# A two-layer decoder on one core: the order in which each engine takes the two lanes' pieces

## Chip, cores and metric

One core of a Trainium2 chip runs the whole program in one launch. Time is device microseconds of that core. The kernel before took 1565.3 us (median of 3 runs, 1559.88 to 1567.16).

## What is computed

Four sequences (batch 4, 512 tokens, width 128, float32) go through six sub-layers, each followed by a residual and a layer norm:

```python
x = _layernorm(x + mamba(x, ...))             # 256 channels, 16 states, scan over 512 tokens
x = _layernorm(x + cross_attention(x, ctx))   # 16 heads, 32 context tokens
x = _layernorm(x + experts(x, ...))           # shared + top 2 of 8 experts, hidden width 512
x = _layernorm(x + window_attention(x, ...))  # 16 heads of 8, band of 128, rotary
x = _layernorm(x + cross_attention2(x, ctx))
x = _layernorm(x + local_layers(x, ...))      # two layers: windows of 64, 8 heads of 64, gated GELU feed-forward of width 341
```

## The kernel before

The four sequences are handled by two *lanes* of code, lane 0 and lane 1. Each has its own scratch, its own four of the eight PSUM banks and its own semaphores. Each lane does two sequences one after the other, called row 0 and row 1 of the lane. So at any time two sequences are under way, and the engines work for both.

For each engine there is one generator per stage and lane: `mamba_*`, `cross_*`, `experts_*`, `window_*`, `cross_*` again and `local_*` twice (l = 0 and 1), with `_tensor` (TensorE, "pe"), `_scalar` (ScalarE, "act"), `_vector` (VectorE, "dve") and `_pool` (GpSimd). `row_sync` issues the loads and stores of a lane from the sync queue ("sp"). Each `yield` ends a *piece*: mostly one operation with the waits ahead of it, sometimes a handful. Over the whole program the two lanes have 806 and 840 pieces on TensorE, 665 and 666 on ScalarE, 836 and 869 on VectorE, 91 and 90 on GpSimd, 43 and 33 on the sync queue.

An engine executes its instructions in the order in which they are written. `interleave` writes that order: it reads `TURNS[engine]`, takes so many pieces of lane 0, then so many of lane 1, and so on:

```python
lanes, done = (first, second), object()
last = [next(lanes[k % 2], done) for k, n in enumerate(turns) for _ in range(n)]
```

Inside a lane the order of the pieces is fixed. Between the lanes it is only `TURNS`. The waits (`wait_ge`) stand inside the pieces, so the data is right under any order that doesn't lock up, but an engine whose next instruction waits does nothing for the other lane either.

Places that the sections below name by line:

- Lane 1 begins with the set-up: `setup_tensor` (L545, L549, and L557, L566, L574, L579 for the folded products of the cross attentions), `setup_vector` (L499, L506, L518, L520 copy the results out, L526 to L535 make constants and tables).
- `mamba_tensor`: projections L684, L688, L694, L701, L708, then for each of 16 states L720 (spread B and C) and L731 (sum). `mamba_vector`: L826 (scale by the root), L837 and L839 (convolution), L847 to L855 (split of B and C in three parts), L859 to L864 (step sizes), then for each state L875 (product) and twice L883 (scan). `mamba_scalar`: L784 (Exp), L787 (Ln), L804 (Exp of each state), L811.
- `local_tensor`: projections L1541, transposes L1430, scores L1582 and L1584, L1597 (transposed weights), L1614 and L1616 (heads), L1549 and L1558 (out). Then the feed-forward: L645 (transposes, in a helper that every stage uses), L1627 (mean), L1630 (mean of squares), L1637 and L1640 (gate and value, three pairs), L1644 and L1652 (down). `local_scalar`: L1522 and L1523 (hT), L1725 (Square), L1727 (Ln), L1730 (Exp), L1736 (Gelu). `local_vector`: L1830 and L1831 scale the normed rows.

Of the kernel before, what the change touches and what calls it, by code (L numbers as in the profile page):

```python
# [103 lines left out]
        5, 21, 4, 3, 1, 10, 2, 5, 4, 4, 2, 1, 6, 2, 3, 3, 3, 3, 3, 3, 5, 3, 3, 3, 3, 3, 3, 3, 3, 5, 3, 3, 3, 3,  # L104
        2, 4, 1, 2, 1, 6, 4, 2, 3, 1, 4, 1, 6, 1, 1, 3, 2, 11, 1, 2, 1, 1, 2, 2, 4, 1, 4, 11, 15, 1, 1, 2, 2, 2,
        3, 5, 6, 6, 6, 1, 1, 17, 17, 1, 3, 1, 1, 9, 3, 6, 2, 3, 3, 1, 11, 5, 1, 2, 3, 1, 2, 5, 6, 6, 6, 6, 6, 6,
        6, 6, 1, 6, 3, 6, 3, 1, 5, 3, 6, 3, 1, 5, 5, 6, 6, 4, 5, 2, 2, 6, 2, 7, 1, 2, 5, 4, 4, 2, 4, 4, 3, 4, 1,
        1, 2, 5, 6, 1, 2, 7, 6, 1, 2, 3, 6, 2, 1, 2, 4, 5, 2, 2, 1, 4, 7, 3, 2, 2, 1, 4, 2, 2, 2, 4, 6, 2, 2, 1,
        2, 5, 2, 4, 3, 3, 1, 2, 1, 1, 1, 1, 1, 2, 1, 1, 5, 2, 2, 3, 3, 2, 1, 3, 5, 1, 2, 7, 6, 2, 2, 2, 5, 2, 2,
        2, 4, 5, 2, 2, 1, 4, 7, 3, 5, 7, 3, 5, 5, 2, 4, 6, 2, 4, 3, 3, 1, 2, 1, 1, 1, 1, 1, 2, 1, 1, 5, 3, 2, 2,  # L110
        3, 5, 4, 1, 1, 4, 4, 4, 1, 1, 5, 2, 3, 3, 3, 3, 3, 3, 3, 3, 3, 3, 3, 3, 5, 3, 3, 4, 3, 1, 1, 2, 2, 1, 3,
        3, 3, 3, 4, 3, 1, 1, 1, 2, 1, 5, 4, 1, 2, 1, 8, 1, 1, 5, 3, 3, 2, 8, 1, 1, 2, 2, 5, 1, 4, 11, 14, 1, 2,
        2, 2, 4, 3, 2, 6, 7, 6, 2, 1, 16, 17, 1, 3, 1, 1, 9, 3, 6, 2, 3, 3, 1, 11, 5, 1, 2, 3, 1, 2, 5, 1, 6, 3,
        6, 3, 1, 2, 5, 4, 1, 3, 3, 2, 2, 1, 1, 3, 3, 2, 2, 1, 1, 3, 3, 2, 2, 1, 1, 5, 3, 1, 3, 3, 3, 2, 2, 1, 1,
        3, 3, 2, 2, 1, 1, 5, 5, 5, 1, 2, 5, 2, 7, 1, 2, 5, 4, 4, 2, 4, 4, 3, 4, 1, 1, 2, 5, 8, 6, 2, 2, 4, 2, 2,
        2, 5, 2, 2, 2, 4, 5, 2, 2, 1, 4, 7, 3, 5, 7, 3, 5, 5, 2, 4, 6, 2, 4, 3, 3, 1, 1, 1, 1, 1, 1, 1, 2, 1, 2,
        3, 3, 2, 2, 1, 2, 1, 3, 3, 1, 1, 3, 1, 4, 6, 6, 2, 2, 2, 5, 2, 2, 2, 4, 5, 2, 2, 1, 4, 7, 3, 5, 7, 3, 5,
        5, 2, 4, 6, 2, 4, 3, 2, 1, 1, 1, 2, 1, 1, 1, 2, 1, 2, 3, 3, 2, 2, 2, 2, 3, 3],
    "act": [
        3, 1, 3, 1, 9, 1, 2, 1, 1, 3, 2, 2, 2, 1, 2, 5, 5, 1, 1, 1, 3, 1, 1, 2, 1, 1, 2, 2, 1, 1, 2, 2, 1, 1, 2,  # L120
        1, 1, 3, 2, 3, 1, 1, 2, 2, 1, 1, 2, 2, 1, 1, 1, 2, 1, 1, 2, 1, 1, 2, 2, 1, 1, 2, 2, 1, 1, 12, 3, 2, 9,
        1, 2, 11, 1, 2, 6, 7, 11, 3, 1, 1, 2, 3, 4, 4, 4, 1, 1, 11, 7, 1, 5, 6, 5, 2, 5, 3, 7, 5, 4, 5, 5, 7, 5,
        4, 7, 5, 4, 12, 5, 4, 5, 5, 7, 5, 4, 7, 5, 2, 3, 2, 6, 14, 3, 1, 3, 2, 3, 3, 3, 3, 2, 5, 4, 1, 5, 3, 3,
        6, 5, 5, 4, 2, 8, 4, 1, 8, 4, 1, 6, 3, 2, 4, 1, 5, 3, 1, 5, 3, 1, 6, 1, 1, 1, 1, 1, 1, 1, 1, 1, 1, 4, 4,
        4, 1, 5, 3, 3, 6, 5, 5, 4, 2, 8, 4, 1, 8, 4, 1, 8, 4, 1, 8, 3, 1, 5, 3, 1, 6, 1, 1, 1, 1, 1, 1, 1, 1, 1,
        1, 4, 4, 2, 1, 3, 1, 2, 3, 1, 2, 3, 1, 1, 3, 1, 2, 5, 1, 1, 1, 2, 1, 1, 2, 1, 1, 2, 2, 1, 1, 3, 2, 1, 1,
# [31 lines left out]
        1, 1, 1, 1, 1, 1, 1, 1, 1, 1, 1, 1, 1, 1, 1, 1, 2, 1, 1, 1, 1, 1, 2, 3, 2, 1, 2, 2, 2, 3, 1, 2, 2, 2, 3,  # L158
        3, 1, 1, 2, 1, 1, 1, 1, 2, 1, 1, 2, 2, 1, 1, 1, 2, 1, 1, 1, 1, 1, 1, 1, 1, 1],
    "sp": [  # L160
        11, 1, 2, 1, 3, 1, 4, 1, 1, 2, 4, 9, 1, 1, 1, 1, 2, 1, 3, 1, 4, 2, 1, 1, 4, 11, 2],
}


# [1968 lines left out]
```

## Time and profile before

| | us |
|---|---|
| median of 3 runs (lowest, highest) | 1565.3 (1559.88, 1567.16) |
| span of the profiled execution, first to last instruction | 1544.1 |
| TensorE busy | 1269.2 (82%) |
| VectorE busy | 1046.3 (68%) |
| ScalarE busy | 808.2 (52%) |
| GpSimd busy | 395.7 (26%) |

For the profiled execution the profile gives the span alone; what a run has around it (start and end of the program) isn't in it. The median is 21.2 us longer than that span. The stages of lane 0 in row 0 begin, by TensorE's first instruction of each, near 13 (Mamba), 203 (cross attention), 248 (experts), 351 (window attention), 494 (second cross attention), 527 and 661 us (local layers); row 1 begins near 800 us. Lane 1 enters Mamba at 68 us and the same later stages 5 to 26 us after lane 0, in the last layer of row 1 1 us before it. A busy TensorE isn't one at full speed: the clock granted to it is given beside it as a share of 2.4 GHz, and 0.5 is its lower level.

### The profile page before, as it was taken

To read this page: it belongs to the slowest core of one execution; us is meant where nothing else is said; L and a number is where in the kernel's file an instruction comes from. 1 tells how busy PE (TensorE), PEld (TensorE's weight loads), DVE (VectorE), ACT (ScalarE), POOL (GpSimd) and SP (SyncE) were. 2 spreads that over 40 slices of the span, in tenths; PEclk is the share of its full clock that TensorE was granted. 3 is DMA by queue.
4 is the path that set the end of the run, shared out by engine and by line. 5 is a ranking of instruction groups with operands and counts; after the bars stand their busy time and mean duration, and the time that the engine had idled before them with its cause. 6 is when DMAs were issued, how large, how long until landed. Compare 5 with 4: busy or idle time off the path is not lost. (4 is left out here: it accounts for less than half of the span.)

```text
span 1544.1 us, 23279 instructions
## 1 busy us (share of the span) xinstructions
PE 1269.2 (82%) x8400; PEld 815.4 (53%) x8400; DVE 1046.3 (68%) x2162; ACT 808.2 (52%) x2180; POOL 395.7 (26%) x248
## 2 busy tenths in 40 slices
PE   5767878887998888789775888889689988988986
PEld 4412335884665556456531233579456654655663
DVE  4789976226887787378449998741378879746853
ACT  2466423453764556466627553336276636665663
POOL 0036633412000332032011665360400023202300
PEclk9789978997999989999987888989799999999997
DMA  8300001780000100001010000068400000000000
GB/s 298 123 0 1 0 1 54 254 268 19 2 1 1 35 21 15 1 15 28 2 28 0 1 0 1 1 201 263 130 1 2 1 1 22 22 1 14 22 8 14
DMA packets 42179, 72.21 MB, mean 47 GB/s; under 512 B 3793, under 2 KB 27473, under 8 KB 41810
## 3 DMA queue, kind: packets, MB, share of 16 engines
q1 hardware_dynamic: 28242, 56.30, 10.8%
q10 hardware_dynamic: 11776, 10.23, 2.6%
q0 software_dynamic: 2048, 4.20, 0.9%
q8 instruction: 68, 1.11, 0.3%
q14 instruction: 45, 0.37, 0.1%
HBM read 51.19 MB, written 13.24 MB: 42 GB/s over the span
## 5 line engine op out<-in xcount | busy, mean ns | idle before, releaser
L912 POOL TENSOR_TENSOR scratch<-scratch 128x1024 f32<-128x1024 f32 x64 | 149.7, 2353 | 140.4 <-DVE scratch L883 119.9
L634 POOL TENSOR_TENSOR small<-small,w_const 128x16 f32<-128x16 f32 x32 | 101.1, 3163 | 298.2 <-DVE small L1753 298.2
L731 PE MATMUL psum<-scratch,w_const 128*128 128x512 f32 x256 | 148.8, 713 | 18.5 <-POOL scratch L912 18.4
L883 DVE TENSOR_TENSOR_SCAN scratch<-psum,scratch 128x512 f32<-128x512 f32 x128 | 150.1, 1206 | 9.5 <-ACT psum L804 8.9
L634 POOL TENSOR_TENSOR rstd<-rstd,w_const 128x4 f32<-128x4 f32 x32 | 32.8, 1029 | 432.9 <-DVE rstd L596 430.3
L1706 ACT ACTIVATE scratch<-psum,mx 128x128 f32<-128x128 f32 x256 | 90.0, 376 | 72.7 <-DVE mx L1794 71.5
L804 ACT ACTIVATE psum<-scratch,a_neg 128x512 f32<-128x512 f32 x128 | 87.8, 690 | 61.2 <-DVE scratch L883 52.1
L1374 ACT ACTIVATE scratch<-psum,mx 128x256 f32<-128x256 f32 (+1 forms) x256 | 111.2, 465 | 10.0 <-DVE mx L1410 8.4
L720 PE MATMUL psum<-scratch,cb 96*128 96x512 bf16 x128 | 49.7, 428 | 60.6 <-DVE scratch L875 51.3
L1160 ACT ACTIVATE scratch<-psum,scratch 128x128 f32<-128x128 f32 x240 | 68.3, 368 | 54.7 <-PE psum L1101 54.6
L1541 PE MATMUL psum<-w_local,hT 128*128 128x512 f32 x192 | 91.2, 615 | 6.3 <-ACT hT L1523 5.1
L731 PEld LDWEIGHTS psum<-scratch,w_const 128*128 128x128 f32 x256 | 53.5, 221 | 79.7 <-issue 45.2
L1243 DVE COPY scratch<-psum 128x128 f32<-128x128 f32 x60 | 17.4, 291 | 109.1 <-PE psum L1115 109.1
L875 DVE TENSOR_TENSOR scratch<-scratch,psum 128x1024 f32<-128x1024 f32 x64 | 76.4, 1198 | 4.0 <-PE psum L720 3.7
L1794 DVE TENSOR_REDUCE mx<-psum 128x4 f32<-128x512 f32 x64 | 44.0, 689 | 51.2 <-PE psum L1584 51.1
L1101 PE MATMUL psum<-scratch,expert_weights 128*128 128x128 f32 x480 | 65.5, 280 | 15.3 <-DMA expert_weights<-in_expert_weights 10.8
L1410 DVE TENSOR_REDUCE mx<-psum 128x4 f32<-128x1024 f32 (+1 forms) x56 | 67.9, 1216 | 9.1 <-PE psum L1321 9.1
L720 PEld LDWEIGHTS psum<-scratch,cb 96*128 96x128 bf16 x128 | 13.4, 105 | 114.0 <-DVE scratch L875 75.4
L1584 PE MATMUL psum<-scratch 64*64 64x128 f32 x512 | 71.7, 281 | 0.0
L1582 PE MATMUL psum<-scratch 64*64 64x128 f32 x512 | 71.7, 281 | 0.0
L1303 PE MATMUL psum<-w_const,scratch 128*128 128x128 f32 x448 | 69.4, 284 | 0.9 <-DVE scratch L1400 0.9
L1101 PEld LDWEIGHTS psum<-scratch,expert_weights 128*128 128x128 f32 x480 | 58.2, 192 | 20.1 <-DMA expert_weights<-in_expert_weights 14.1
(266 smaller groups left out, 3199.6 us busy)
## 6 DMA issues: line engine op xcount, KB each, us to landing
expert_weights<-in_expert_weights SPq DMA_DIRECT2D x61, 512.0 KB, 5.1
scratch<-scratch ACTq DMA_DIRECT2D x48, 128.0 KB, 2.3
folded_products<-expert_weights SPq DMA_DIRECT2D x8, 512.0 KB, 3.1
folded<-folded_products SPq DMA_DIRECT2D x8, 512.0 KB, 4.7
w_local<-in_local SPq DMA_DIRECT2D x1, 3122.0 KB
sorted_y<-scratch ACTq DMA_DIRECT2D x12, 256.0 KB, 5.6
scratch<-sorted_x SPq DMA_DIRECT2D x4, 704.0 KB, 6.7
scratch<-in_cross SPq DMA_DIRECT2D x1, 2624.5 KB, 12.9
```

Source lines behind the costliest of these rows:

```text
L634: t.eng.tensor_tensor(v, v, W("const", "neg_half").to_broadcast([P, v.shape[1]]), ALU.pow).then_inc(t.s[done], 1)
L731: ins = pe.matmul(sum_banks[c], ident, t.m.hC[:, 2 * ((n - 1) % 2) + c, :], start=(n == 1), stop=(n == NS))
L804: act.activation(t.ps["dA"], t.m.delta[:, c, :], ACT.Exp, scale=a_neg[:, c, n:n + 1])\
L875: dve.tensor_tensor(t.m.dBu[n % 2], t.m.du[:, :, :], bank, ALU.mult).then_inc(t.s["v_freed"], 1)
L883: dve.tensor_tensor_scan(t.m.hs[:, n % 2, c, :], t.ps["dA"], t.m.dBu[n % 2][:, c, :], 0.0, ALU.mult, ALU.add)\
L912: t.eng.tensor_tensor(t.m.hC[:, 2 * (n % 2):2 * (n % 2) + 2, :], t.m.hs[:, n % 2], C, ALU.mult)\
L1101: ins = pe.matmul(tok(bank, f), t.m.weights[b % BUFS][:, f * P:(f + 1) * P], tok(t.m.xsT, b), start=(f == 0), stop=(f == NF - 1), skip_gro ...
L1374: ins = act.activation(t.m.wide_pr[:, n % 2, u, z], bank[:, z], ACT.Exp, bias=t.m.mx2[:, c:c + 1], accum_out=t.m.sums2[:, c:c + 1])
L1541: pe.matmul(ring.open(), tok(t.m.hT, i), w_qkv[:, c * 512:(c + 1) * 512], start=True, stop=True).then_inc(t.s[sig], 1)
L1582: pe.matmul(own[0:64, :], qs[:, 0:64], ks[:, q - before:q - before + P], start=False, stop=False, skip_group_check=True)
L1584: ins = pe.matmul(own[64:P, :], qs[:, 64:P], ks[:, q:q + P], start=False, stop=(g == 3), skip_group_check=True)
L1706: ins = act.activation(tok(t.m.pr[:, u, :], a), tok(bank, a), ACT.Exp, bias=t.m.mx2[:, c:c + 1], accum_out=t.m.sums2[:, c:c + 1])
```

## The change

All five lists of `TURNS` are replaced. The new ones were made by a procedure that goes through time and lets each engine take, of the pieces that are ready, the one with the longest chain of work behind it, with a preference between the lanes that depends on the stage. The kernel holds only its result. The pieces, their instructions, waits, buffers and banks are as before. The lists add up to the same number of pieces for each lane. The number of runs (entries) goes from 511 to 738 for "pe", 435 to 604 for "act", 714 to 894 for "dve", 131 to 132 for "pool" and 27 to 36 for "sp". The first entries of each list, before and after:

```diff
--- before.py
+++ after.py
 TURNS = {
     "pe": [
-        5, 21, 4, 3, 1, 10, 2, 5, 4, 4, 2, 1, 6, 2, 3, 3, 3, 3, 3, 3, 5, 3, 3, 3, 3, 3, 3, 3, 3, 5, 3, 3, 3, 3,
-        2, 4, 1, 2, 1, 6, 4, 2, 3, 1, 4, 1, 6, 1, 1, 3, 2, 11, 1, 2, 1, 1, 2, 2, 4, 1, 4, 11, 15, 1, 1, 2, 2, 2,
-        3, 5, 6, 6, 6, 1, 1, 17, 17, 1, 3, 1, 1, 9, 3, 6, 2, 3, 3, 1, 11, 5, 1, 2, 3, 1, 2, 5, 6, 6, 6, 6, 6, 6,
...
+        5, 34, 4, 1, 1, 4, 2, 3, 1, 1, 3, 1, 5, 2, 3, 3, 3, 3, 3, 3, 2, 1, 1, 2, 5, 3, 3, 3, 2, 1, 1, 2, 2, 2,
+        1, 3, 3, 2, 1, 1, 2, 3, 3, 3, 2, 3, 1, 3, 1, 5, 1, 1, 4, 1, 5, 1, 1, 3, 1, 1, 1, 1, 4, 3, 2, 1, 1, 7, 1,
+        2, 1, 1, 6, 1, 1, 3, 1, 3, 2, 5, 9, 2, 1, 1, 2, 1, 2, 1, 2, 3, 2, 1, 1, 1, 1, 3, 2, 1, 1, 1, 3, 1, 1, 4,
...
     "act": [
-        3, 1, 3, 1, 9, 1, 2, 1, 1, 3, 2, 2, 2, 1, 2, 5, 5, 1, 1, 1, 3, 1, 1, 2, 1, 1, 2, 2, 1, 1, 2, 2, 1, 1, 2,
-        1, 1, 3, 2, 3, 1, 1, 2, 2, 1, 1, 2, 2, 1, 1, 1, 2, 1, 1, 2, 1, 1, 2, 2, 1, 1, 2, 2, 1, 1, 12, 3, 2, 9,
...
+        4, 2, 5, 1, 4, 2, 1, 2, 2, 1, 1, 1, 1, 3, 2, 2, 1, 1, 4, 1, 1, 2, 3, 2, 1, 1, 3, 1, 2, 2, 2, 1, 1, 2, 2,
+        2, 1, 2, 1, 1, 1, 2, 1, 1, 2, 3, 1, 1, 2, 2, 1, 1, 3, 3, 2, 1, 1, 2, 2, 1, 1, 1, 1, 1, 1, 1, 1, 1, 1, 1,
...
     "dve": [
-        6, 12, 1, 1, 1, 8, 4, 1, 1, 1, 1, 1, 1, 1, 1, 4, 1, 3, 1, 3, 2, 1, 3, 5, 4, 5, 1, 1, 1, 3, 2, 1, 1, 1,
-        2, 1, 1, 2, 2, 1, 1, 2, 2, 1, 1, 2, 2, 1, 1, 1, 1, 1, 1, 1, 1, 2, 2, 1, 1, 2, 2, 1, 1, 2, 1, 1, 1, 2, 1,
-        1, 2, 2, 1, 1, 2, 2, 1, 1, 2, 2, 1, 1, 1, 4, 1, 2, 2, 2, 1, 1, 1, 1, 2, 1, 1, 1, 2, 1, 4, 1, 3, 1, 2, 1,
...
+        7, 20, 1, 15, 3, 2, 6, 1, 1, 1, 1, 1, 1, 1, 3, 5, 2, 1, 1, 3, 2, 1, 1, 1, 1, 1, 1, 2, 1, 1, 2, 1, 1, 1,
+        1, 1, 2, 2, 1, 1, 1, 1, 1, 1, 1, 1, 1, 1, 1, 1, 1, 1, 2, 2, 1, 1, 1, 1, 1, 2, 2, 1, 1, 1, 1, 1, 1, 1, 1,
+        1, 1, 1, 1, 1, 1, 1, 1, 1, 1, 1, 1, 1, 1, 1, 1, 1, 1, 1, 1, 4, 1, 3, 2, 1, 1, 1, 1, 2, 2, 1, 2, 1, 1, 1,
...
     "pool": [
-        3, 2, 5, 1, 1, 1, 1, 1, 1, 1, 1, 1, 1, 1, 1, 1, 1, 1, 1, 1, 1, 1, 1, 1, 1, 3, 2, 1, 1, 1, 2, 2, 1, 1, 1,
...
+        3, 2, 4, 1, 1, 1, 1, 1, 1, 1, 1, 1, 1, 1, 1, 1, 1, 1, 1, 1, 1, 1, 1, 1, 1, 1, 1, 3, 1, 1, 2, 2, 2, 1, 1,
...
     "sp": [
-        11, 1, 2, 1, 3, 1, 4, 1, 1, 2, 4, 9, 1, 1, 1, 1, 2, 1, 3, 1, 4, 2, 1, 1, 4, 11, 2],
+        10, 1, 2, 1, 1, 1, 5, 2, 2, 1, 1, 2, 3, 5, 1, 2, 2, 2, 1, 1, 1, 1, 5, 1, 2, 1, 1, 2, 1, 1, 2, 1, 1, 6,
+        2, 2],
 }
```

## Rows read from the trace of the kernel before

**Rows 1.** The page: busy us of each engine; TensorE's busy tenths and clock in slices

```profile
PE 1269.2 (82%) x8400; PEld 815.4 (53%) x8400; DVE 1046.3 (68%) x2162; ACT 808.2 (52%) x2180; POOL 395.7 (26%) x248
...
PE   5767878887998888789775888889689988988986
...
PEclk9789978997999989999987888989799999999997
```

**Rows 2.** Busy time by stage: stretch, its length, then the engines, clock, DMA share, GB/s

```profile
64.00:192.00 128.00, 94.12 (x219) 35.07 (x220) 118.52 (x116) 74.42 (x117) 69.06 (x31) 0.89 0.02 9
...
192.00:260.00 68.00, 52.33 (x201) 30.22 (x200) 47.42 (x136) 21.00 (x34) 21.39 (x17) 0.80 0.00 1
...
351.00:371.00 20.00, 14.61 (x44) 8.56 (x44) 10.77 (x59) 4.07 (x7) 8.22 (x9) 0.57 0.10 27
...
371.00:496.00 125.00, 117.95 (x1066) 80.14 (x1067) 98.51 (x269) 81.82 (x305) 1.01 (x1) 1.00 0.01 2
...
496.00:532.00 36.00, 29.00 (x134) 17.43 (x133) 26.26 (x75) 12.68 (x22) 11.40 (x11) 0.91 0.05 15
...
787.00:806.00 19.00, 9.84 (x38) 5.61 (x37) 10.10 (x40) 4.39 (x18) 4.55 (x6) 0.73 0.20 55
...
806.00:950.00 144.00, 109.30 (x243) 41.27 (x242) 134.49 (x132) 81.63 (x123) 70.20 (x30) 0.81 0.00 0
...
1102.00:1121.00 19.00, 13.39 (x40) 8.04 (x41) 10.31 (x56) 2.99 (x5) 8.34 (x9) 0.55 0.11 28
...
1121.00:1247.00 126.00, 119.33 (x1076) 80.61 (x1073) 97.96 (x272) 80.81 (x307) 1.01 (x1) 1.00 0.01 1
```

**Rows 3.** The same view in steps of 10 us, local layers of row 0

```profile
630.00:640.00 10.00, 5.86 (x21) 2.74 (x20) 1.66 (x3) 6.84 (x11) 0.00 (x0) 1.00 0.01 2
...
640.00:650.00 10.00, 6.78 (x10) 2.85 (x11) 3.29 (x6) 4.54 (x6) 0.00 (x0) 0.66 0.00 0
...
760.00:770.00 10.00, 3.90 (x11) 1.33 (x9) 2.15 (x4) 7.69 (x11) 0.00 (x0) 0.91 0.00 0
```

**Rows 4.** Timeline of TensorE, row 0's first local layer: start us, us, what

```profile
629.40 0.66 PE L645 MATMUL psum<-w_const,x 128*128 128x128 f32 x4
...
643.22 2.07 PE L1637 MATMUL psum<-scratch,w_local 128*128 128x512 f32 x2 [5.18 <-DVE scratch L1831]
...
655.01 1.02 PE L1640 MATMUL psum<-scratch,w_local 128*128 128x512 f32 x2
```

**Rows 5.** Chain of waits in the last local layer: start us, us, what

```profile
1497.49 0.60 PE psum L645 x4
...
1503.22 0.59 ACT hT L1523
...
1503.83 1.28 ACT L1727
...
1509.68 2.08 PE psum L1637 x2
```

**Rows 6.** Groups of ScalarE by form: line, operation, count, busy us, mean ns

```profile
L1727 ACT ACT_TABLE_LOAD x6 | 7.7, 1283 | 0.1
...
L771 ACT ACT_TABLE_LOAD x1 | 1.3, 1283 | 0.0
```

**Rows 7.** Timeline of TensorE at the start

```profile
37.80 3.53 PE L694 MATMUL psum<-scratch,w_mamba 128*8 128x512 f32 x4
...
43.14 1.98 PE L708 MATMUL psum<-scratch,w_mamba 8*128 8x512 f32 x4
...
58.33 1.05 PE L579 MATMUL psum<-scratch,expert_weights 128*128 128x128 f32 x8
```

**Rows 8.** Timeline of VectorE at the start

```profile
43.25 0.69 DVE L847 CAST scratch<-psum 96x512 bf16<-96x512 f32 x1 [4.66 <-PE psum L701]
...
63.94 0.27 DVE L535 TENSOR_SCALAR w_rows<-w_rows,gate 1x128 f32<-1x128 f32 x1
```

**Rows 9.** Timeline of all engines between row 0 and row 1

```profile
800.05 1.08 PE L645 MATMUL psum<-w_const,y 128*128 128x128 f32 x4 [8.22 <-DVE y L826]
```

105 rows, old and new, of the table TURNS are left out of this document.

## The prediction

> **What bounds the kernel now.** I read the page first [rows 1]: TensorE is busy for 1269.2 of 1544.1 us and VectorE for 1046.3. No engine is full over the whole span, so the question is where TensorE's missing 274.9 us lie. The digits show them in the first eighth, just past the middle, and in notches between stages. The windows cut by stage say why [rows 2]. In the first Mamba stretch VectorE works 118.5 of 128 us and in the second 134.5 of 144: VectorE is the bound there, and no order of turns wins more than its idle 9.5 us in each. In row 0's window attention TensorE works 118.0 of 125 us at full clock: 7 us to win. The idle sits in the seams: 15.7 of 68 us around the first cross attention, 5.4 of 20 and 5.6 of 19 us where lane 0 has begun the window attention and lane 1 has not (there the granted clock is 0.57 and 0.55, close to the lower level of 1.2 GHz, because TensorE has one lane's chain alone), 7 of 36 us around the second cross attention, and 9.2 of 19 us between row 0 and row 1.
>
> Finer windows [rows 3] show the same in the gated feed-forward at the end of each local layer: 5.9 of 10 us busy, then 6.8 at a clock of 0.66; in the second layer 3.9 of 10. The timeline of TensorE [rows 4] shows both lanes there at once: lane 0's transposes (L645) start at 629.40, but its first matmul of the feed-forward (L1637) only at 643.22, and takes 2.07 us a pair where a later pair of that width takes 1.02. The chain of waits in the last layer [rows 5] gives such a chain almost undisturbed: 1497.49 to 1509.68, 12.2 us of short steps with two table loads in it. All this is latency of two lanes standing in the same narrow place together.
>
> **What the change does to the order.** No instruction is altered, so I merged the two lanes' pieces by both tables and named each piece by its line. The number of runs goes from 511 to 738 on TensorE, 714 to 894 on VectorE, 435 to 604 on ScalarE, 131 to 132 on GpSimd and 27 to 36 on the sync queue. A turn costs no instruction. What counts is how far the lanes are shifted. Summing the traced busy time of lane 1's pieces that stand ahead of each lane 0 piece, the two orders differ by at most 8 us on TensorE outside the last layer and by 12 to 16 us within it. It is the same plan with small shifts, so I expect tens of microseconds at the very most.
>
> **Start.** Before, TensorE does 21 set-up pieces, then lane 0's projections L694 to L708, then the rest. After, all 34 set-up pieces come first. On VectorE 14 of the 35 set-up pieces used to be mingled with lane 0's L847 to L864; now all come ahead of them. TensorE's set-up ends at 58.33 + 1.05 = 59.4 [rows 7]; lane 0's projections (37.80 to 43.14 + 1.98 = 45.12, 7.3 us) leave it, so it ends near 52, and L694 slips from 37.80 to 52: 14 us later. VectorE's set-up ended at 63.94 + 0.27 = 64.2 [rows 8] with about 9 us of lane 0's work inside; now near 57. Lane 0's L847 slips from 43.25 to 57, its first scan from 65 to about 72, and lane 1 starts 7 us sooner. From 57 on VectorE has 118.5 + 9 = 127.5 us to do plus some 6 us of idle while both chains start (before, it idled 9.5): 57 + 127.5 + 6 = 190.5 against 192. I take -1 us; bounds -7 (no idle) and +14 (the slip of L694 isn't made good).
>
> **First cross attention and experts.** After, lane 1 is 4 to 8 us of work further on when lane 0 enters, so the two chains run beside each other rather than one after the other. The idle is 15.7 us in row 0 [rows 2]; I take a quarter of it, -4, and -1 for row 1, where the lanes were closer already. Bounds: 0 and -16. The lone-lane stretch before lane 1's window attention follows from lane 1's lag: it enters the experts about 4 us sooner, worth its idle share and the slow clock, -3 in row 0 and -1 in row 1. Bounds: +5 and -11 (both idles).
>
> **Window and second cross attention.** Here 1.7 to 6.4 us less of lane 1's work stands ahead of lane 0's pieces, so its latency-bound cross attention lies beside lane 1's last window units. Idle is 7 us around it [rows 2]: -2 in each row, bounds 0 and -7. Where TensorE was already full, finer turns give nothing.
>
> **Feed-forward of the local layers.** This is the largest shift. In row 0's first layer seven of lane 1's attention pieces (5.4 us on TensorE) that stood ahead of lane 0's L645 now stand behind it, inside lane 0's 12.2 us chain; then lane 0's 10.4 us of L1637 to L1652 stand inside lane 1's chain. Worked from the start of L645: it moves from 629.4 to 624. Chain 12.2, lane 0's matmuls with lane 1's three short pieces 10.4 + 2.8, a rest of lane 1's chain not covered 1.5, lane 1's matmuls 10.4 with lane 0's six projections of the next layer 6.1 between them: 624 + 12.2 + 13.2 + 1.5 + 16.5 = 667.4, where before the same work was done near 670.3. So -3 for each first layer, -6 in all, and -3 for row 0's second. At the start of a layer both lanes' rotations fill VectorE while TensorE waits; with the lanes apart I take -3 for all four layers together. Bounds for these: 0, and -22 (the idle of the four feed-forwards and their slow clock, about 5.5 us each).
>
> **Between the rows.** TensorE waits 8.22 us for lane 0's L826 [rows 9]: store, load, root. After, lane 0 leaves the layer with about a seventh of lane 1's feed-forward pieces still to come, so most of that wait has work beside it: -5, bounds 0 and -8.
>
> **The end.** Before, both lanes end together. After, lane 1 has 8 to 12 us of TensorE work more behind lane 0, and its last chain of 12.2 us has only 2.7 us of its own matmuls in it and nothing of lane 0. Before, the two lanes' steps lay in it together, and by the like stretches of [rows 3] 4 to 6 us of it were idle. I take +3, bounds 0 and +9.
>
> **Table loads.** The load rows [rows 6] add up to 39 (twelve rows from x6 to x1), 1.283 us each. A load stands wherever the set of functions changes between Exp, Silu, Ln and the two Gelus. That rule, run over the old order, gives exactly 39 at the same lines; over the new one 46: L1727, L1730 and L1736 go from 16 to 24, the Mamba lines lose one. 7 x 1.283 = 9.0 us more on ScalarE. It is busy for only 808.2 of 1544.1 us, and the added loads are lane 1's, while TensorE has lane 0's next projections: I take +2 on the path, bounds 0 and +9.
>
> The Trainium skill speaks against this part: "ScalarE: Activation LUTs", section "Table sets: the hidden batching unit", says to group activations by set, and its section "What ACT_TABLE_LOAD costs" adds a drain of about 1.38 us to the 1.28. By that price the seven would be an estimated 18.6 us instead of 9.0. The trace agrees on 1.28 and shows no drain: L1523 ends at 1503.22 + 0.59 = 1503.81 and the load starts at 1503.83 [rows 5].
>
> **Sum.** -1 - 5 - 4 - 4 - 6 - 3 - 3 - 5 + 3 + 2 = -26 us. A fixed order stalls wherever an instruction waits and the other lane's ready work is queued behind it; 227 more changes of lane on TensorE give more such places. The trace can't show stalls of an order that hasn't run; bounds 0 and +26 (all gain lost). I take +8, nearer to 0, since the order before also came with such stalls. Net -18. The profiled span of 1544.1 becomes 1526; the median of the runs, 1565.3, lies 21.2 us over that span, which I keep: 1547 us, 1.2% faster.
>
> **The rivals.** (a) *Seams filled wholly*: each seam term at its far bound. 16 + 11 + 14 + 22 + 8 would be 71 us; two thirds of it, 47, with start, end and loads as forecast (+4) gives -43: 1522. For: the idle is there and the lanes move apart where it lies. Against: the shifts are only a few us. Chance 0.13. (b) *No change*: the two Mamba stretches and the window stretch of each row (128 + 144 + 125 + 126 us [rows 2]) have little to give, and new stalls eat the seams: 1565, chance 0.2. (c) *Lane 0 held at the start*: every lane 0 piece behind L694 runs 14 us late, because all 34 set-up pieces come first. It decides if VectorE runs dry between 57 and 75 and lane 0 stays the lane that ends the Mamba stretch; then +14 there, and with the seams giving only 4: 1575. For: the slip of L694 is certain. Against: lane 1 gains 7 us and VectorE was idle 9.5 us in that stretch anyway. Chance 0.12. (d) *Loads on the path*: each added load delays the chain it stands in, 9.0 us, and stalls take the rest of the gain: 1574. By the price of a switch in the Trainium skill ("ScalarE: Activation LUTs", "What ACT_TABLE_LOAD costs") it would be about 1584, an estimate. Chance 0.07. My forecast has 0.48.
>
> **How the numbers follow.** A change under 0.5% (7.8 us) can't be told from none here. The forecast's own range is 1530 to 1557; (a) lies below it, (b) within, (c) and (d) above. Faster: 0.48 + 0.13, plus a little of (b): 0.62. Slower: (c) and (d): 0.19. Same: 0.19. Range 1518 to 1576.
>
> **What would show it.** Right: 46 table loads; L694 near 52 us; TensorE above 8 of 10 us busy in the first layer's feed-forward and at clock 1.0; the 8.22 us wait before row 1 under 4; TensorE's busy time nearly the same or slightly less, as fewer matmuls run at the lower clock. Wrong: the first row's Mamba stage ends past 200 us; or waits of TensorE on VectorE and ScalarE in the window attention grow by more than 10 us; or the lone-lane windows keep their 20 us.

## The result, and the profile after

| | kernel before | changed kernel |
|---|---|---|
| median of the runs made together, us | 1562.6 (1557.29 to 1567.16, 4 runs) | 1516.9 (1510.01 to 1518.27, 4 runs) |
| span of the profiled execution, us | 1544.1 | 1516.5 |

The ratio is 0.971, 95% interval 0.967 to 0.975: 2.9% faster, 46 us, where I had forecast 18 (1547 us, 1.2%). The time lies 1 us below the range of 1518 to 1576. The medians in this document count every run, but ratios leave out the few that took over 1.5% longer than their kernel's quickest. The profiled execution of the changed kernel took 1518.27 us, so only 1.8 us lie around its span of 1516.5.

The page of the changed kernel, the lines that answer to [rows 1]: busy us of each engine, TensorE's tenths and clock.

```profile
PE 1243.7 (82%) x8400; PEld 807.8 (53%) x8400; DVE 1040.7 (69%) x2162; ACT 814.1 (54%) x2187; POOL 396.7 (26%) x248
...
PE   5667779796899889889875777869689987989896
...
PEclk9789978897999999998997999789899999999998
```

The page shows that the instructions are the same but for seven more on ScalarE (46 table loads for 39). TensorE is busy 25.5 us less (1243.7 for 1269.2) for the same 8400 matmul instructions, so some of them ran faster. No stage time can be read off the page; the windows and the timelines below give them.

The changed kernel in steps of 10 us around lane 0's first feed-forward, as in [rows 3]:

```profile
620.00:630.00 10.00, 8.64 (x77) 6.50 (x74) 3.95 (x7) 6.86 (x23) 0.00 (x0) 1.00 0.00 1
630.00:640.00 10.00, 8.28 (x61) 4.81 (x60) 4.12 (x9) 7.79 (x10) 0.00 (x0) 1.00 0.01 2
...
750.00:760.00 10.00, 6.60 (x61) 4.30 (x59) 3.69 (x8) 6.77 (x9) 0.00 (x0) 0.99 0.01 2
```

TensorE works 8.64 and 8.28 of 10 us at clock 1.0, as I had named for this place (before: 5.86, then 6.78 at 0.66), and 6.60 in the second layer's step that had 3.90.

Its timeline of TensorE there, which answers to [rows 4]: L663 is the old L645, L1655 and L1658 the old L1637 and L1640.

```profile
624.73 0.66 PE L663 MATMUL psum<-w_const,x 128*128 128x128 f32 x4
...
634.13 1.13 PE L1576 MATMUL psum<-w_local,scratch 128*128 128x128 f32 x8 [0.78 <-ACT scratch L1702]
635.10 1.02 PE L1655 MATMUL psum<-scratch,w_local 128*128 128x512 f32 x2
635.96 1.02 PE L1658 MATMUL psum<-scratch,w_local 128*128 128x512 f32 x2
636.82 0.60 PE L663 MATMUL psum<-w_const,x 128*128 128x128 f32 x4
```

Lane 0's chain from its transposes to its first product takes 10.4 us instead of 13.8. The wait of 5.18 us at its end is gone, since lane 1's attention (L1576) stands there, and a pair takes 1.02 us instead of 2.07. Lane 1's transposes come only at 636.82, inside lane 0's products. This is what the prediction described; it was right in kind and too small in size.

### The profile page after: what moved, and what is told of

The parts are those of the page before. It is cut to its first block, busy times and chain, and to the rows that moved or that the text cites. A ratio compares the mean times of both kernels' runs of the same rounds, so it can differ in the third digit from the quotient of the medians.

```text
span 1516.5 us, 23285 instructions
## 1 busy us (share of the span) xinstructions
PE 1243.7 (82%) x8400; PEld 807.8 (53%) x8400; DVE 1040.7 (69%) x2162; ACT 814.1 (54%) x2187; POOL 396.7 (26%) x248
## 3 DMA queue, kind: packets, MB, share of 16 engines
q1 hardware_dynamic: 28242, 56.30, 11.1%
## 4 chain that ended last, share of the span: by engine, by line
PE 46%; DVE 23%; ACT 15%; issue 8%; POOL 3%; DMA 3%; ACTq 1%; SPq 1%; another core or an unknown queue 0%; POOLq 0%; DVEq 0%
DVE scratch L901 6%; PE psum L1339 3%; PE psum L1119 3%; PE psum L1358 3%; DVE scratch L893 3%; PE psum L1133 3%; PE psum L1321 3%; PE psum L1600 3%; ACT scratch L1724 3%; PE psum L1559 2%; PE psum L1334 2%; PE psum L749 2%; PE psum L1632 2%; PE psum L956 2%; PE psum L1448 1%
## 5 line engine op out<-in xcount | busy, mean ns | idle before, releaser
L749 PE MATMUL psum<-scratch,w_const 128*128 128x512 f32 x256 | 137.5, 664 | 9.8 <-POOL scratch L930 9.8
L749 PEld LDWEIGHTS psum<-scratch,w_const 128*128 128x128 f32 x256 | 49.3, 206 | 59.1 <-issue 38.8
L1119 PE MATMUL psum<-scratch,expert_weights 128*128 128x128 f32 x480 | 68.7, 293 | 10.4 <-issue 5.4
L1321 PE MATMUL psum<-w_const,scratch 128*128 128x128 f32 x448 | 64.2, 282 | 8.1 <-DVE scratch L1418 6.7
L1119 PEld LDWEIGHTS psum<-scratch,expert_weights 128*128 128x128 f32 x480 | 62.9, 207 | 13.5 <-issue 8.9
```

The lines of the kernel that those rows point to most:

```text
L749: ins = pe.matmul(sum_banks[c], ident, t.m.hC[:, 2 * ((n - 1) % 2) + c, :], start=(n == 1), stop=(n == NS))
L1119: ins = pe.matmul(tok(bank, f), t.m.weights[b % BUFS][:, f * P:(f + 1) * P], tok(t.m.xsT, b), start=(f == 0), stop=(f == NF - 1), skip_gro ...
L1321: ins = pe.transpose(tok(bank, c), tok(t.m.wide_pr[:, n % 2, u, :], c), ident)
```

## The experiments

The two orders pass through common points: places where both have issued the same pieces of both lanes. At such points I cut both tables and spliced them, so that a kernel has the new order in some stretches and the old in the rest. The stretches are: start (set-up, Mamba, first cross attention), experts, window (with the second cross attention), local, then Mamba with the cross attention of row 1, experts, window and local again. Ratios are to the kernel before, from runs on the same chip; its medians in the five groups of runs were 1564.6, 1571.0, 1562.1, 1563.1 and 1564.0 us. Starts of stages are those of lane 0's first TensorE instruction in each.

**One stretch at a time.**

```diff
 TURNS = {  # spliced; stretches in order: start experts window local | Mamba experts window local
+  new local layers alone:      old old old NEW | old old old NEW
+  new experts alone:           old NEW old old | old NEW old old
+  new start alone:             NEW old old old | old old old old
+  all new but the experts:     NEW old NEW NEW | NEW old NEW NEW
+  new window alone:            old old NEW old | old old NEW old
+  new experts and local:       old NEW old NEW | old NEW old NEW
```

New local layers alone.

> The new order in the local layers of both rows alone (from lane 0's first piece of them to its first Mamba piece of row 1, and to the end); the order before everywhere else. Theory 1 (the two traces set side by side: lane 0 gains 19 us over row 0's local layers and the seam behind them, the last stage 14 us or so over row 1's): about -30 us, ratio 0.98. Theory 2 (the sizes that the prediction gave these parts, -6 -3 -3 -5 +3 +2): -12 us, ratio 0.992. Rival: the local order gains only when the lanes arrive shifted by what stands ahead of it: -5 to 0 us.

New experts alone.

> The new order in the experts of both rows alone. Theory 1 (traces: lane 0 enters the experts 4 us earlier after the change and leaves them 8 us later; about the same in row 1, 16 us earlier and then 11): slower by 8 to 12 us a row, ratio 1.010 to 1.015. Theory 2 (the prediction's lone-lane term): 4 us faster, ratio 0.997. Rival: the loss comes from where the lanes stand when they arrive, not from the order inside: no change.

New start alone.

> The new order from the start to lane 0's first experts piece alone (set-up first, Mamba, first cross attention of row 0). Theory 1 (traces: lane 1 is 13 us ahead at its Mamba and both lanes 4 to 6 us ahead at the experts): -5 us, ratio 0.997. Prediction: -1 -4 = -5 as well. Rival (c) of the prediction, lane 0 held back by the set-up: +14 us, ratio 1.009.

All new but the experts.

> The new order everywhere but in the experts of both rows, where the order before stands. If the experts' new order costs 8 to 12 us a row (theory 1), this is 15 to 20 us faster than the changed kernel: some 1500 us, ratio 0.96 to the kernel before. If it costs nothing (rival), it is at the changed kernel's 0.971. If the stages' gains don't add, because the seams between the two orders cost, it is slower than 0.971.

New window alone.

> The old order with only the two stretches from the start of the window attention to the end of the second cross attention in the new order. By the stage times of the changed kernel these stretches take 173 and 171 us against 175.5 and 173. Theory A (the gain stays when the stretch is alone): 4 to 6 us faster, ratio 0.996 to 0.998. Theory B (the shift pays only together with the lag that the new experts' order brings): no change, ratio 0.999 to 1.003. Forecast of the prediction for these stretches: -4 us in all.

New experts and local layers.

> The new order in the experts and in the local layers alone, the rest old. The new local layers alone gave 1526 us, the new experts alone 1563 (nothing), all but the experts 1534, everything 1517. Theory A (the experts' gain of 4 to 8 us a row is real but is given back in the Mamba and cross stages behind them where these stay old): 1520 to 1527 us, the experts' stages 113 to 116 us by the profile, Mamba and first cross of row 1 at 198 to 201 us as with the new experts alone. Theory B (it is lost again in the local layers' old order): 1508 to 1517.

| new order in | median us (runs) | ratio, 95% interval |
|---|---|---|
| local layers | 1526.5 (6) | 0.974, 0.969 to 0.979 |
| experts | 1563.0 (12) | 1.001, 0.997 to 1.005 |
| start | 1563.3 (12) | 1.000, 0.997 to 1.004 |
| window | 1563.6 (10) | 0.996, 0.992 to 1.000 |
| all but experts | 1533.6 (6) | 0.980, 0.976 to 0.984 |
| experts and local | 1537.7 (4) | 0.982, 0.977 to 0.987 |
| everything | 1516.1 and 1514.3 (4 and 5) | 0.965, 0.960 to 0.970 and 0.968, 0.964 to 0.973 |

Three things follow. The local layers alone bring most of the gain, 38 us by the medians and 41 by the ratio. I had thought from one trace that the new experts' order costs 8 to 12 us a row; that fell, alone it costs nothing. And the parts do not add up. The new experts' order is worth nothing by itself (1.001), but some 17 us when all the rest is new: the kernel with all but the experts takes 1533.6 us, clear of the changed kernel's 1514 to 1517. Beside the new local layers alone it may even cost something (0.982 against 0.974), though the two intervals just overlap. The windows of the kernel with new experts and local layers, stretch and length first, then the engines, clock, DMA share and GB/s, show each row's experts at 115 us, 3 less than with the new local layers alone (118 and 118):

```profile
251.00:366.00 115.00, 92.45 (x682) 83.70 (x681) 31.62 (x157) 46.95 (x144) 35.00 (x35) 0.90 0.61 195
797.00:994.00 197.00, 147.11 (x406) 63.79 (x407) 173.23 (x226) 98.96 (x156) 89.50 (x47) 0.85 0.01 3
994.00:1109.00 115.00, 88.74 (x664) 79.34 (x663) 31.04 (x157) 46.54 (x143) 33.29 (x33) 0.90 0.63 195
```

But the experts start 3 us later (251 for 248), the window stretch behind them takes 178 for 175 and row 1's Mamba and cross attention (the middle line) 197 for 191: 12 us given back, perhaps because these stretches expect another lag between the lanes. In the changed kernel the Mamba stretch takes 193 behind the same experts. That fits the mechanism of theory A of that run but doesn't show it, since the same stretch in the old order took 189 to 196 us behind the old experts' order too; the median, 1537.7, is above both theories' numbers. How each stretch hands its lag on was not taken apart further, nor which of the four compute engines' new orders carries the gain in the local layers.

The new start was expected to give 5 us and gave none that can be told; the new window order lies between its two theories (0.996, up to 1.000).

**The kernel before, profiled again.** No edit.

> The kernel before, unchanged, for a second profiled execution of it. The profiled execution that the prediction was worked from had a span of 1544.1 us; the runs of the kernel before had spans of 1553 to 1576 us at granted clocks of 0.90 to 0.915. Theory A (the profiled execution was a fast one in the two experts' stages, where the weights of the experts come in): from the start of the experts to the start of the window attention this one takes 112 to 120 us in row 0 and 112 to 120 in row 1, where the first took 103 and 106, every other stage is within 3 us of the first profile, and the span is 1555 to 1568. Theory B (the whole execution was evenly faster, by its clock): the difference is spread over all stages in proportion to their TensorE work, under 5 us in the experts.

Ratio 0.999 (0.996 to 1.003), profiled execution 1577.60 us, its span 1575.8: again 1.8 apart. Theory A holds in kind: the difference sits in the experts' stages, and every other stage is within 2 us of the first profile. Row 1's 123 us and the span lie above its numbers. The experts' stages (first and third line) and the local layers (second and fourth) of the first profile:

```profile
248.00:351.00 103.00, 88.61 (x683) 79.58 (x682) 34.59 (x160) 49.20 (x146) 34.21 (x34) 0.98 0.67 218
527.00:800.00 273.00, 224.44 (x1805) 148.23 (x1803) 173.50 (x286) 156.15 (x455) 55.00 (x21) 0.92 0.08 20
996.00:1102.00 106.00, 90.15 (x672) 81.04 (x670) 31.75 (x157) 48.47 (x144) 33.67 (x34) 0.95 0.65 211
1275.00:1544.00 269.00, 222.91 (x1803) 147.94 (x1801) 172.49 (x281) 160.24 (x451) 53.83 (x19) 0.93 0.06 15
```

The same kernel's second profile:

```profile
248.00:368.00 120.00, 97.51 (x687) 87.12 (x688) 33.29 (x160) 49.29 (x146) 34.44 (x34) 0.91 0.58 187
542.00:815.00 273.00, 224.37 (x1806) 148.46 (x1806) 173.50 (x286) 156.34 (x455) 55.00 (x21) 0.92 0.08 20
1010.00:1133.00 123.00, 102.87 (x676) 92.30 (x675) 32.49 (x160) 48.36 (x144) 33.80 (x34) 0.85 0.56 182
1307.00:1576.00 269.00, 222.52 (x1800) 147.65 (x1798) 172.40 (x280) 160.43 (x451) 53.83 (x19) 0.93 0.06 15
```

And the changed kernel:

```profile
244.00:359.00 115.00, 94.91 (x676) 85.45 (x676) 31.88 (x159) 47.02 (x144) 34.73 (x35) 0.88 0.60 195
532.00:786.00 254.00, 221.71 (x1806) 147.26 (x1805) 172.53 (x281) 163.78 (x461) 54.47 (x21) 0.95 0.08 20
979.00:1091.00 112.00, 90.57 (x664) 82.05 (x665) 30.93 (x158) 46.44 (x143) 33.10 (x33) 0.91 0.63 200
1262.00:1516.00 254.00, 216.68 (x1806) 143.51 (x1805) 172.54 (x282) 163.14 (x453) 53.75 (x19) 0.96 0.07 16
```

The local layers take 273 and 269 us in both profiles of the kernel before, to the microsecond. The experts take 103 and 106 in one, 120 and 123 in the other: some 33 us of the same code, with the clock and the GB/s both lower in the slower one. The other kernels with the old experts' order had 107 to 122 us a row, and the changed kernel 112 to 122 in three profiles. So the profile that I worked from was an unusually quick execution in just those two stages: its span of 1544.1 us lies under the spans of all timed runs beside these experiments, 1552.7 us or more. The second profile is of a long execution (1577.60 us, where the median beside it is 1571.0). Against the second profile the change gives, stage by stage from lane 0's first TensorE instruction: start 4, experts 5, window 1, local 19, Mamba 2, experts 11, window 3, local 14, together the 59 us between the spans. That is more than the 46 to 55 us between the medians, and of the stages only the local layers are clear of their spread: 269 to 273 us in both profiles of the kernel before, 251 to 254 in three profiles of the changed one.

**The sync queue alone.** The changed kernel with the experts' stages of "sp" in the old order, and the old kernel with the new "sp".

```diff
 "pe", "act", "dve", "pool": new          "pe", "act", "dve", "pool": old
-"sp": 36 runs (new)                     -"sp": 27 runs (old)
+"sp": old in both experts' stages       +"sp": 36 runs (new)
```

> The changed kernel with the sync queue's two experts' stages in the old order: lane 0's sorted_x load is no longer queued behind lane 1's four weight loads, which wait for lane 1's routing. Theory A (the new queue order holds lane 0's experts up: TensorE waited 7.33 us for sorted_x in row 0): 5 to 14 us faster than the changed kernel, about 1505 to 1512. Theory B (the stage's end is set by the experts' weights arriving, and sorted_x has slack): within 4 us of the changed kernel. Theory C (what the new order gains in the experts, 14 us between the kernel with all but the experts new and the changed kernel, comes from lane 1's weights being asked for earlier): 8 to 14 us slower than the changed kernel, about 1528.

> The old order on the four compute engines, the new order on the sync queue alone (36 runs for 27). The mirror image of the changed kernel with the old queue, which lost 54 us. Theory A (the queue's order has to match the order in which the other engines come to the blocks; a load that stands behind another lane's block waits for it, and holds all behind it): slower than before, by 10 to 60 us. Theory B (the new queue order is better by itself): 5 to 15 us faster than before.

The first took 1570.1 us (0.998, 0.995 to 1.001), 54 more than the changed kernel beside it (1516.1): the whole gain. The second took 1593.5 us (1.022, 1.017 to 1.027), 31 more than the kernel before, inside its theory A. For the first my theories A, B and C all fell short; C had the direction. Its waits of TensorE and of the sync queue (SPq) in row 0's experts; sorted_x holds the tokens sorted by expert. Line, what was waited for, us in total, times, longest.

```profile
PE psum L1122 <- DMA expert_weights<-in_expert_weights: 20.9, 5, 8.4
PE psum L1091 <- ACT scratch L1155: 13.4, 1, 13.4
PE psum L1108 <- DMA scratch<-sorted_x: 8.2, 1, 8.2
...
SPq L1925 <- DVE scratch L1264: 71.8, 15, 13.2
```

The same in the changed kernel:

```profile
PE psum L1105 <- DMA scratch<-sorted_x: 7.3, 1, 7.3
...
PE psum L1119 <- DMA expert_weights<-in_expert_weights: 1.9, 1, 1.9
...
SPq L1922 <- DVE scratch L1261: 30.3, 13, 7.3
```

Both lanes' weight loads stand in one queue. Each lane has four buffers for the weights, and a load waits until the block that used its buffer has been copied out (the VectorE line). In an order that isn't the one in which the engines come to the blocks, a load waits for a block that is not due yet, and the other lane's loads wait behind it: 71.8 us instead of 30.3 (31.3 in the kernel before, where both orders are old), and the stage takes 157 us instead of 115. So the 36 numbers of "sp" cost 31 us by themselves, and leaving their experts' part old costs 54 us beside the rest.

**Two neighbours swapped.** In the changed order lane 1's four first loads, which wait for its routing, stand ahead of lane 0's sorted_x. The swap, twice run:

```diff
-"sp": [10, 1, 2, 1, 1, 1, 5, 2, ... 2, 2, 2, 1, 1, 1, 1, 5, ...
+"sp": [10, 1, 3, 2, 5, 2, ... 2, 2, 2, 2, 2, 5, ...
```

> The changed kernel with two neighbours swapped on the sync queue in each row: lane 0's sorted_x load ahead of lane 1's four first weight loads, the rest of that queue as changed. TensorE waits 7.3 and 7.7 us for that load in the profiles of the changed kernel. Theory A (that wait is on the path): 5 to 14 us faster than the changed kernel, 1503 to 1511 us, TensorE's wait for sorted_x gone. Theory B (the stage runs at the pace of the weight loads, each of which waits for a block to be copied): the wait moves to the weights, within 4 us of the changed kernel. Theory C (the old place of that load is what cost 54 us when the whole queue had its old order): above 1540.

> The changed kernel again, on the same chip as the other kernels of this comparison: ratio 0.967 to 0.975 to the kernel before (1510 to 1525 us). Expected by both theories on the experts; it is the mark that the kernel with the old sync queue is read against.

> The changed kernel with lane 0's sorted_x load ahead of lane 1's first weight loads, once more and beside the changed kernel on one chip. Theory A (the wait for sorted_x was on the path, 5 us of each row's experts' stage): 6 to 10 us faster than the changed kernel here too, its experts' stages at 107 to 110 us against 112 to 116. Theory B (the first look was a fast execution of a stage that varies by itself): within 3 us.

> The changed kernel again, beside the one with the two neighbours swapped on the sync queue: 1510 to 1520 us, ratio 0.965 to 0.971.

1508.8 and 1507.4 us (4 runs each), against 1516.1 and 1514.3 for the changed kernel; made side by side, 1507.4 against 1514.3. The difference of 7 us is inside theory A's 5 to 14, though the ratios' intervals overlap (0.966, 0.960 to 0.971; 0.968, 0.964 to 0.973), so the gain is likely and not shown. The experts' stages of the swapped kernel, 111 and 109 us:

```profile
244.00:355.00 111.00, 91.28 (x673) 82.33 (x671) 31.48 (x157) 47.11 (x144) 34.52 (x34) 0.90 0.62 202
972.00:1081.00 109.00, 89.60 (x665) 81.22 (x666) 30.90 (x157) 46.54 (x143) 33.38 (x33) 0.92 0.64 206
```

The wait for sorted_x (15.1 us in two waits in the changed kernel) is gone from them. A part comes back at L1122, the first matmul of a block, which needs its weights: in row 0 TensorE stands there for 8.7 us where the profile names nobody that it waits for, against 2.7 us in the changed kernel.

```profile
PE psum L1122 <- issue: 8.7, 4, 6.0
```

It is the quickest kernel of this study.

**The chain ahead of the feed-forward, shortened.** Both orders with the norm's Ln and Exp replaced, so the kernel leaves its root out. There are eight such chains, not the sixteen that the expectation names.

```diff
-act.activation(t.m.rst, t.a.take(), ACT.Ln, bias=eps)...
+act.activation(t.m.rst, t.a.take(), ACT.Identity, bias=eps)...
-act.activation(t.m.rst, t.m.rst, ACT.Exp, scale=-0.5)...
+act.activation(t.m.rst, t.m.rst, ACT.Copy, scale=-0.5)...
```

> The kernel before, with the two functions of the local layers' norm replaced (Ln by Identity, Exp by Copy), which leaves the root out and shortens the chain ahead of each feed-forward by its two table loads, 2.6 us in each of 16 chains, and takes most of the 39 loads away. Theory A (what the change recovers is the latency of those chains, which stand bare in the old order and beside the other lane's work in the new): at least 25 us faster than before (4 layers by 2.6 and more, with TensorE's clock held up), and the distance to the changed kernel with the same edit shrinks from 47 to 54 us to under 35. Theory B (the distance comes from lane 0 having its way in the attention part, not from the chains): 10 to 20 us faster than before, distance still above 42.

> The changed kernel with the same two functions replaced (the root left out), which takes most of its 46 table loads away. Forecast of the prediction: the seven added loads cost 2 us on the path. Theory A (chains are covered in the new order): under 15 us faster than the changed kernel, 1502 to 1515. Theory B (loads are on the path as much as before): as much faster as the kernel before gets by the same edit.

The old order took 1545.0 us (0.990, 0.987 to 0.994), 17 less than before. The new took 1522.7 (0.970, 0.964 to 0.977; 1509.9 to 1533.6, 4 runs), no less than the changed kernel: the distance shrinks from 46 us or more to 31 by the ratios, 22 by the medians. Since row 1's experts took 125 us in the profile of the second, I compare the local layers. The old order without the root:

```profile
536.00:800.00 264.00, 218.88 (x1804) 144.56 (x1804) 172.89 (x284) 150.65 (x451) 55.01 (x21) 0.95 0.08 21
1283.00:1541.90 258.90, 215.52 (x1804) 143.86 (x1802) 172.57 (x281) 149.95 (x443) 53.84 (x19) 0.96 0.06 15
```

The new order without it:

```profile
533.00:783.00 250.00, 217.72 (x1805) 144.05 (x1803) 172.00 (x281) 151.13 (x451) 54.38 (x21) 0.97 0.08 20
1273.00:1523.00 250.00, 213.82 (x1805) 141.16 (x1803) 172.40 (x281) 150.44 (x443) 53.75 (x19) 0.97 0.07 16
```

542 falls to 523 us in the old order, 508 to 500 in the new: 19 and 8. In two more profiles of the changed kernel these layers took 503 and 504, so the 8 may be 3. The new order covers more than half of what the same edit shows as bare latency in the old. Theory A is right in kind, for the distance; for the size, the 17 us lie in theory B's range. 23 of the 34 us between the local layers stay, so the chains' table loads aren't all of it.

**TensorE kept from standing still.** Extra products ahead of each feed-forward, ten or three; each is two matmul instructions.

```diff
+                bank = t.a.open()
                 if c == 0:
+                    for _ in range(FILL):
+                        pe.matmul(bank, mean_w, t.m.hT[:, :], start=True, stop=True)
                     t.w(t.s["hn_ready"])
-                pe.matmul(t.a.open()[0:m, :], w1[...], t.m.hc, start=True, stop=True)
+                pe.matmul(bank[0:m, :], w1[...], t.m.hc, start=True, stop=True)
```

> The kernel before with ten extra matmuls (128x512, the same product ten times into the bank that the next matmul opens anyway) on TensorE where it waits for hn_ready ahead of each feed-forward: 160 more, 35 to 45 us of TensorE work, in its idle time only if the other lane has nothing there. They keep TensorE from standing still. Theory A (about half of what the new order gains in the local layers comes through the clock: matmuls behind an idle stretch ran at 1.2 GHz): the feed-forward's matmuls (L1637 to L1652) fall from 14 to 21 us a lane and layer to 10 to 13 at a granted clock of 1.0, and the kernel is 0 to 15 us faster than before although work is added. Theory B (the clock is a side effect and the idle time itself is the loss): the matmuls don't get shorter by more than 1 us, and the kernel is 10 to 30 us slower.

> The kernel before with three extra products (two matmul instructions each, 0.44 us an instruction by the run with ten) ahead of each of the eight feed-forwards, 2.6 us a chain and 21 us in all, so that both lanes' fillers together just fit the 5.2 us in which TensorE waits for hn_ready. With ten, the matmuls L1637 fell from 846 to 596 ns, but 70 us were added and the kernel lost 40. Theory A (part of the local layers' loss in the old order is the clock, and it comes back when TensorE does not stand still): 0 to 12 us faster than before, clock 0.92 or more in the profile against 0.90. Theory B (the clock costs nothing on the path): 2 to 15 us slower.

> The changed kernel with the same three extra products a chain. Here the other lane's work stands in the chain and the clock is up. Both theories: 8 to 21 us slower than the changed kernel, 1524 to 1538. If it is less than 5 us slower, then the chains stand bare in the new order as well, and theory A of the run without the root is in doubt.

With ten, the old order took 1603.3 us (1.027): 70 us of work were added where I had reckoned 35 to 45, and 40 of them reach the time, which lies beyond both theories, though L1637 fell from 846 to 596 ns as theory A has it. With three, 21.9 us were added. The old order took 1561.8 us (0.998, 0.994 to 1.001), no longer than without them; the new took 1539.3 (0.982, 0.975 to 0.989), 22 to 25 us more than the changed kernel by the medians and 17 to 27 by the ratios. The changed kernel did not run beside it; 8 to 21 were expected. The groups of L1637 and L1640 with 128 rows, count, busy us, mean ns and the idle time ahead: the kernel before in its second profile,

```profile
L1637 PE MATMUL psum<-scratch,w_local 128*128 128x512 f32 x32 | 23.8, 846 | 14.6 <-DVE scratch L1831 14.6
L1640 PE MATMUL psum<-scratch,w_local 128*128 128x512 f32 x32 | 20.1, 716 | 0.0
```

the same order with three fillers (L1642 is the fillers),

```profile
L1642 PE MATMUL psum<-hT,w_const 128*128 128x512 f32 x48 | 21.9, 592 | 0.0
L1644 PE MATMUL psum<-scratch,w_local 128*128 128x512 f32 x32 | 18.4, 661 | 5.2 <-DVE scratch L1838 5.2
L1647 PE MATMUL psum<-scratch,w_local 128*128 128x512 f32 x32 | 18.2, 654 | 0.0
```

and the changed kernel:

```profile
L1655 PE MATMUL psum<-scratch,w_local 128*128 128x512 f32 x32 | 16.8, 607 | 2.7 <-DVE scratch L1849 2.7
L1658 PE MATMUL psum<-scratch,w_local 128*128 128x512 f32 x32 | 16.6, 599 | 0.5 <-DVE scratch L1859 0.4
```

The old order takes 21.9 us of added work for nothing: at these two groups 9.4 us of idle time are used (14.6 to 5.2), and the products behind them are 7.3 us shorter (43.9 to 36.6). Its local layers, fillers included, take 271 and 266 us at a clock of 0.96 and 0.97, where they took 273 and 269 at 0.92 and 0.93:

```profile
545.80:817.10 271.30, 227.55 (x1825) 148.31 (x1825) 172.87 (x284) 155.79 (x455) 55.02 (x21) 0.96 0.08 20
1303.50:1569.70 266.20, 224.42 (x1825) 148.93 (x1824) 172.28 (x280) 160.09 (x451) 53.84 (x19) 0.97 0.06 15
```

The new order has little of either to give: the same fillers lengthen its local layers by 17 and 6 us, in row 0 at a clock of 0.92 for 0.95, which I can't explain. So of what the change gains at these two groups, 10.5 us are shorter products (43.9 to 33.4), which the fillers tie to the clock (33.1 in the old order with ten of them), and 11.4 the wait (14.6 to 3.2).

## Why the prediction was wrong

**The base, wrong.** "The median of the runs, 1565.3, lies 21.2 us over that span, which I keep." In every execution profiled since, 1.8 us lie around the span. The other 19.4 were work: the profiled execution was quick in the two experts' stages, where the second profile, itself a long one, spends 33 us more. Those microseconds are not a constant to be added to the end; they sit in a stage that the change touches. By its own profile the changed kernel shows 27.6 us less than [rows 1]'s span, near my gross -26, but only since this profile pays the common experts' time and the other didn't.

**The feed-forward, start of layers, between the rows and the end: -6 -3 -3 -5 +3 = -14; found -19 and -14, together -33.** This is the mis-sized term, and the main one. I had traced one chain per layer and found -3. Two things were left out of the sum. The first is the clock: [rows 4] showed a pair at 2.07 us for 1.02, I quoted it, and worked on with 10.4 us of products a lane in both orders. Summed by lane from the traces, lane 0's own L1637 to L1652 kept TensorE busy for 10.0 to 12.2 us in the old order and 9.5 to 9.7 in the new; all eight feed-forwards together, both lanes, for 89.3 and 77.5. From the first of them to the last, lane 0 took 15.7 to 21.0 us in the old order and 11.1 to 11.4 in the new; that also holds lane 1's work in between, so only part of it is clock. The second is the attention part ahead of it: in the first layer of both rows lane 0 comes through it in 92.5 us instead of 102 and 96, and the lanes then stand 16 us apart instead of 7 and 1. Lane 0's second chain, too, is 10.4 us long in both rows, for 13.8 and 13.1. How much of the gain the lag alone is worth was not measured. The far bounds, -22 and -8, together are short of it too. The wait between the rows went nearly as forecast, from 8.22 [rows 9] to 4.08 us, just not under 4:

```profile
785.67 1.09 PE L663 MATMUL psum<-w_const,y 128*128 128x128 f32 x4 [4.08 <-DVE y L844]
```

The end cost nothing that shows; in lane 1's last chain only 1.35 us are bare:

```profile
1485.51 0.60 PE L663 MATMUL psum<-w_const,x 128*128 128x128 f32 x4
...
1495.68 1.13 PE L1655 MATMUL psum<-scratch,w_local 128*128 128x512 f32 x2 [1.35 <-DVE scratch L1849]
```

It lasts 10.2 us where [rows 5] had 12.2, the products behind it 1.13 for 2.08.

**The stalls of an order that hasn't run, +8: the size by luck.** One new stall was there, and not at TensorE's changes of lane, from which I had argued the term: the wait for sorted_x behind lane 1's weight loads, 7.3 and 7.8 us where the kernel before waits 2.3 in one row, worth some 7 us by the swap. No other is seen in any stage.

**Cross attention and experts, -4 -3 -1 -1.** The first cross attention went as forecast: lane 0 spends 40.7 us in it for 44.6 in row 0, and 35.6 for 37.2 in row 1. The stretch in which lane 0 is alone in the window attention fell from 20.3 and 19.5 us in the first profile, 18.3 and 19.2 in the second, to 16.3 and 17.7. Against the second profile the experts gave 5 and 11 us, but alone they gave nothing; with everything else new they are worth some 17. I had priced the sync queue's order at nothing; it is worth 54 us to this kernel. That was an edit I named (27 runs to 36) and didn't cost.

**Start, -1: not contradicted.** TensorE's first projection came at 47.27 (forecast near 52, [rows 7]) and lane 0 still ends row 0's Mamba stage at 191; alone the start, with the first cross attention, changed nothing (1.000, 0.997 to 1.004).

```profile
46.29 1.05 PE L597 MATMUL psum<-scratch,expert_weights 128*128 128x128 f32 x8
47.27 1.88 PE L712 MATMUL psum<-scratch,w_mamba 128*8 128x512 f32 x4
```

**Window, -2 and -2:** by the profiles -1 and -3; alone 0.996 with an interval that reaches 1.

**Table loads: 46, as the rule said.** The three groups of the feed-forward have eight each, 24 for the 16 of before:

```profile
L1745 ACT ACT_TABLE_LOAD x8 | 10.3, 1283 | 0.1
...
L1748 ACT ACT_TABLE_LOAD x8 | 10.3, 1283 | 0.1
...
L1754 ACT ACT_TABLE_LOAD x8 | 10.3, 1283 | 0.1
```

ScalarE is busy 5.9 us more. Whether the +2 on the path was right isn't separated; without the norm's two functions the new order's local layers gain 3 to 8 us, the old order's 19. The Trainium skill ("ScalarE: Activation LUTs", "Table sets: the hidden batching unit") would have the order group the functions by set; here the finer order has seven more loads, 9.0 us, and is 46 us faster.

**The rivals.** (a), seams filled wholly at 1522 us, was the nearest, 5 us off, with a chance of 0.13. Its number is partly luck: it took two thirds from every seam alike, and the local layers gave 33 us where their far bounds were 30, while the window seams gave 4 of 14. Its argument against, "the shifts are only a few us", was the mistake: a few us of TensorE work are enough to put one lane's products into the other's chain. (b), (c) and (d) did not happen.

**The signs.** The loads, TensorE's share and clock in the feed-forward and its lower busy time came as named; the first projection came 5 us earlier than "near 52" and the wait between the rows missed its bound by 0.08 us. No sign of being wrong came: TensorE's waits on VectorE and ScalarE in the window attention stayed within 4 us of the old ones. The signs tested the kind of the change and not its size.

## What to carry to other kernels

Compare the profiled span with several runs before reading a sum off it, and if they differ, look for the stage that varies; here it was the one fed by DMA. Where two chains stand bare beside each other, count the wait and also the slower products behind it: here, at the two groups of products behind the chain, they were worth about the same. An order of a queue is priced only together with the orders of the engines that release its entries.

## What was not expected of the hardware

The same program spent 103 and 106 us in its experts' stages in one execution, 120 and 123 in another. In row 0 the two part at the clock: in the first 14 us with expert weights under way it was 0.90 in the one and 0.74 in the other, and 80 against 51 matmul instructions went through. The window 262 to 276 us of the first profile of the kernel before, then of its second:

```profile
262.00:276.00 14.00, 13.22 (x80) 10.28 (x79) 9.71 (x47) 3.43 (x6) 11.56 (x12) 0.90 0.61 210
```

```profile
262.00:276.00 14.00, 11.90 (x51) 9.16 (x51) 5.65 (x32) 2.16 (x4) 10.86 (x11) 0.74 0.65 221
```

The queue's loads then come later: lane 1's first ones at 276.5 and 281.8 us. Why the clock differs between executions of one program at the same place stays open, as does what else moves the experts' time of one order between 103 and 123 us.

21.9 us of added matmuls cost nothing in one order of the same instructions and some 22 us in the other.
